# The feed-forward part of a gated state-space block in a new order on all engines

## What is computed

```
d_t, B_t, C_t = projections of u = silu(conv(in_proj @ ctx))     # per item
state = state * exp(d_t * A) + (d_t * u_t) * B_t                 # 16 state rows, over 256 positions
y     = (sum over the rows of state * C_t + D * u) * silu(norm(x))
x2    = x + tanh(g_xattn) * y
h     = act_quant(norm(x2))
inter = silu(h @ Wgate') * (h @ Wup')                            # 1024 wide
out   = x2 + tanh(g_ffn) * act_quant(fwht(inter)) @ Wdown'
```

## Time and profile before

| | |
|---|---|
| median of 3 runs | 265.46 us (264.85 to 266.59) |
| the profiled execution | 265.58 us, of which 263.8 us is the span from first to last instruction |
| busy share of the span: PE, DVE, ACT, POOL | 71%, 81%, 60%, 56% |
| mean granted clock of PE | 0.883 of full speed |

### The profile page before, as it was taken

How to read it: one execution, slowest core, us unless ns; L and a number is a source line. 1 busy time by engine, 2 the same in 40 slices (tenths; PEclk the granted TensorE clock), 3 DMA queues, 4 the chain that set the end, 5 groups by cost and what they waited for, 6 DMA issues and landing times. The chain is left out here.

```text
span 263.8 us, 3694 instructions
## 1 busy us (share of the span) xinstructions
PE 187.3 (71%) x1209; PEld 155.8 (59%) x1216; DVE 213.9 (81%) x340; ACT 157.3 (60%) x271; POOL 147.5 (56%) x213
## 2 busy tenths in 40 slices
PE   3779489895595569867667787675596768474945
PEld 2547388794494468647557666564485547342944
DVE  4489997898989499579989897998959775579872
ACT  1685996949234556994776799735748504650040
POOL 1100890999961096039999942999930399008500
PEclk9999855899779559999997999999979988989597
DMA  3891000000000000000000000000000000000001
GB/s 60 268 363 75 1 4 0 0 1 2 0 0 2 0 0 1 2 1 0 0 2 0 0 20 4 20 4 0 0 0 24 0 20 2 0 0 1 20 22 40
DMA packets 8149, 6.34 MB, mean 24 GB/s; under 512 B 2202, under 2 KB 7874, under 8 KB 8130
## 3 DMA queue, kind: packets, MB, share of 16 engines
q1 hardware_dynamic: 7154, 6.02, 7.1%
q10 hardware_dynamic: 976, 0.09, 0.3%
...
...
## 5 line engine op out<-in xcount | busy, mean ns | idle before, releaser
L1105 POOL TENSOR_SCALAR driveT<-duT,BT 128x256 f32<-128x256 f32 x120 | 62.2, 538 | 41.0 <-issue 21.3
L823 ACT ACTIVATE decay<-delta,zero_c,aneg 128x255 f32<-128x255 f32 x128 | 65.2, 589 | 1.7 <-DVE delta L1254 1.6
L1230 DVE TENSOR_TENSOR_SCAN state<-decay,BC 128x512 f32<-128x512 f32 x30 | 36.4, 1213 | 4.4 <-issue 4.3
L1272 DVE TENSOR_TENSOR prod<-state,BC 128x1024 f32<-128x1024 f32 x32 | 38.5, 1204 | 0.6 <-issue 0.6
L463 PE MATMUL PY<-id,prod 128*128 128x128 f32 x256 | 37.9, 297 | 1.4 <-DVE x L1294 1.0
L1230 DVE TENSOR_TENSOR_SCAN state<-decay,UP 128x512 f32<-128x512 f32 x30 | 35.8, 1193 | 0.0
L463 PEld LDWEIGHTS PY<-id,prod 128*128 128x128 f32 x256 | 32.8, 154 | 2.5 <-issue 1.2
L447 PE MATMUL BC<-bc,sel 96*128 96x256 bf16 x64 | 13.1, 288 | 27.4 <-DVE prod L1272 27.3
L1130 POOL TENSOR_TENSOR wnat<-wnat 128x512 f32<-128x512 f32 x18 | 22.9, 1274 | 15.9 <-DVE wnat L1352 15.2
L933 ACT COPY hT<-GP 128x1024 f32<-128x1024 f32 x8 | 8.1, 1010 | 35.0 <-PE GP L612 35.0
L407 PE MATMUL BC<-id,driveT 128*128 128x128 f32 x120 | 21.2, 305 | 10.9 <-POOL driveT L1105 10.8
...
## 6 DMA issues: line engine op xcount, KB each, us to landing
...
```

What stands on the lines that cost most here:

```text
L823: last = nc.scalar.activation(decay[:, m % RING, h, n, 1:L], delta[:, b % 2, h, 1:L], ACT.Exp, bias=zero_c[:], scale=aneg[:, h, NB * j + n ...
L1105: last = nc.gpsimd.tensor_scalar(driveT[:, m % RING, c, n], duT[:, b % 2, c], BT[:, b % 2, c, NB * j + n:NB * j + n + 1], 1.0, ALU.mult, A ...
L1230: nc.vector.tensor_tensor_scan(state[:, g % STATES, h].rearrange("p n l -> p (n l)"), decay[:, g % RING, h].rearrange("p n l -> p (n l)"), ...
L1272: nc.vector.tensor_tensor(prod[:, g % RING].rearrange("p h n l -> p h (n l)"), state[:, g % STATES].rearrange("p h n l -> p h (n l)"), PC. ...
```

## The change

The order of each engine's loop is written anew; no arithmetic is changed.

- In steps 3 to 5 PE does gate 0, up 0, gate 1, up 1, so `up(f, t)` waits for the silu of its own tile, and `gate(f, 1)` waits for `gate_times_up(f, 0)`. On DVE `gate_times_up(f, 0)` and `(f, 1)` go from the middle of steps 5 and 6 to the end of steps 4 and 5, and POOL's folds from steps 5, 6, 7 to 4, 5, 6.
- `inter_T(f, 0)` goes to PE's step 6, and `hadamard_mm(f, 0)` from step 0 of the next item to step 7. `absmax2(p, 0)` goes from step 1 to step 0, `round_down(p, 0)` from the start of step 2 to that of step 1, `q2_T(p, 0)` from 2 to 1. `hadamard_mm(p, 1)` stands ahead of `C_rows` in step 2, where it stood at the end of the step, and `absmax2(p, 1)` ahead of the scans of step 3, where it stood behind them.
- POOL makes driving terms LEAD = 5 steps ahead; the ring stays at 4. The pieces of `softplus_tail` and two of `weight_scale` stand a little earlier.
- ACT does `rstd2(f)` at the end of step 0 ahead of `softplus`, `copy_duT` in step 3 ahead of `for_silu`, `q2_out_early(p, 1)` between the two silus, `inter_out(f, 0)` in step 6.
- PE does `x_dbl(n)` in step 5, one step earlier, and of `in_proj` for n = 3 one half in step 1 and one in step 2, where they stood in 2 and 3.
- In the tail `absmax2(p, 0)` stands ahead of `residual`, and `round_down`, `q2_out`, `q2_T` of (2, 0) ahead of the tokens of item 3.
- Some PSUM banks and the waits that go with them are others.

The diff, cut to its core (helpers, PE's loop, then ACT's, POOL's, DVE's), shifted to the left:

```diff
+LEAD = 5
...
 def duT_bank(n):
-    return bank4 if n == 1 else X
+    return {1: bank4, 2: bank5}.get(n, X)
 def dt_bank(n):
     return bank5 if n < 2 else X
 def gateT_bank(k):
-    return bank6 if k == 0 else X
+    return bank6 if k <= 1 else X
...
...
         else:
             pe.wait_ge(dve_qT, 1)
         if f == 0 and t == 0:
-            pe.wait_ge(dve_wT, 6)
-            pe.wait_ge(act_duT, 2)
+            pe.wait_ge(act_duT, 3)
         elif f < B - 1 and t == 0:
             pe.wait_ge(act_tq, LC * f)
         elif f < B - 1:
-            pe.wait_ge(act_sg, LC * f + 1)
+            pe.wait_ge(dve_mul, LC * f + 1)
         elif t == 0:
             pe.wait_ge(act_tp, LC * f)
         else:
-            pe.wait_ge(act_tq, LC * f - 1)
+            pe.wait_ge(dve_scan, HALF * B * STEPS)
+            pe.wait_ge(dve_out, LC * (B - 2))
         tokens_by(f, t, wgT, pe_gate)
     def up(f, t):
-        if f == B - 1:
-            pe.wait_ge(act_sg, LC * f + t + 1)
-        elif t == 0:
-            pe.wait_ge(act_sg, LC * f + 2)
-        else:
-            pe.wait_ge(dve_mul, LC * f + 1)
+        pe.wait_ge(act_sg, LC * f + t + 1)
         tokens_by(f, t, wuT, pe_up)
...
         if DVE_DRIVES <= g + 2 < B * STEPS:
             drive_rows(g + 2, 0)
             drive_rows(g + 2, 1)
+        if s == 2:
+            if old:
+                hadamard_mm(p, 1)
         if s == 3:
             if new:
                 tokens_T(f)
-        if s == 4:
-            if new:
-                gate(f, 1)
         if g + 1 < B * STEPS:
             C_rows(g + 1)
         accumulate(g)
         if s == 0:
-            if k == 0:
-                dt_proj(1)
+            if k < B - 1:
+                dt_proj(k + 1)
+            if k == 0:
                 gate_T(0)
-            if 1 <= k < B - 1:
-                dt_proj(k + 1)
-            if old:
-                hadamard_mm(p, 0)
         if s == 1:
             if k == 0:
                 weight_sum()
+            if old:
+                inter_T(p, 1)
             if k >= 1:
                 gate_T(k)
             if old:
-                inter_T(p, 1)
+                q2_T(p, 0)
+            if k == 1:
+                in_proj(n, 0)
         if s == 2:
-            if old:
-                q2_T(p, 0)
             if front:
-                in_proj(n, 0)
-            if old:
-                hadamard_mm(p, 1)
+                in_proj(n, k)
         if s == 3:
-            if k == 0:
-                du_T(1)
+            if k < B - 1:
+                du_T(k + 1)
+            if new:
+                gate(f, 0)
             if old:
                 down(p, 0)
-            if new:
-                gate(f, 0)
-            if front:
+            if k == 0:
                 in_proj(n, 1)
+            if new:
+                up(f, 0)
         if s == 4:
-            if 1 <= k < B - 1:
-                du_T(k + 1)
-            if new:
-                up(f, 0)
             if old:
                 q2_T(p, 1)
+            if new:
+                gate(f, 1)
+                up(f, 1)
         if s == 5:
             if k == 0:
                 weight_T(0)
                 weight_T(1)
-            if new:
-                up(f, 1)
             if old:
                 down(p, 1)
+            if front:
+                x_dbl(n)
         if s == 6:
             if k == 0:
                 weight_T(2)
                 weight_T(3)
-            if front:
-                x_dbl(n)
+            if new:
+                inter_T(f, 0)
         if s == 7:
             if k == 0:
                 weight_T(4)
                 weight_T(5)
             if new:
-                inter_T(f, 0)
+                hadamard_mm(f, 0)
 p, f = B - 2, B - 1
-hadamard_mm(p, 0)
 inter_T(p, 1)
+hadamard_mm(p, 1)
+q2_T(p, 0)
 tokens_T(f)
-hadamard_mm(p, 1)
 gate(f, 0)
-q2_T(p, 0)
 gate(f, 1)
 up(f, 0)
 up(f, 1)
...
                 softplus(1)
                 gate_out(0)
             if new:
-                rstd2(f)
-            if old:
-                quant_down(p, 0)
-            if new:
                 second_norm(f)
         if s == 2:
             if new:
...
                 tokens_out_early(f)
             if old:
                 quant_down(p, 1)
-        if s == 4:
-            if k == 0:
-                copy_duT(1)
-        if s == 5:
-            if old:
-                q2_out_early(p, 1)
-        if s == 7:
-            if front:
-                dt_rows(n)
-                copy_BT(n)
-                high_pieces(n)
         if g + AHEAD < B * STEPS:
             decays(g + AHEAD)
         if s == 0:
+            if old:
+                quant_down(p, 0)
+            if new:
+                rstd2(f)
             if 1 <= k < B - 1:
                 softplus(k + 1)
         if s == 1:
...
             if old:
                 q2_out_early(p, 0)
         if s == 3:
+            if k < B - 1:
+                copy_duT(k + 1)
             if new or k + 1 < B:
                 for_silu()
             if new:
...
                 silu_u(n)
             if k + 1 < B:
                 silu_z(k + 1)
+            if old:
+                q2_out_early(p, 1)
             if new:
                 silu_gate(f, 1)
             for_exp()
-        if s == 4:
-            if 1 <= k < B - 1:
-                copy_duT(k + 1)
+        if s == 6:
+            if new:
+                inter_out(f, 0)
         if s == 7:
-            if new:
-                inter_out(f, 0)
+            if front:
+                dt_rows(n)
+                copy_BT(n)
+                high_pieces(n)
 p, f = B - 2, B - 1
+quant_down(p, 0)
 rstd2(f)
 for_silu()
 second_norm(f)
+inter_out(p, 1)
 scale_tokens(f)
-inter_out(p, 1)
-quant_down(p, 0)
 silu_gate(f, 0)
 quant_down(p, 1)
 silu_gate(f, 1)
...
 last.then_inc(pool_diag, 1)
 drives(DVE_DRIVES)
 norm_z(0)
-for m in range(DVE_DRIVES + 1, AHEAD):
+for m in range(DVE_DRIVES + 1, LEAD):
     drives(m)
 for k in range(B):
     p, f, n = k - 2, k - 1, k + 2
     old, new, front = p >= 0, f >= 0, n < B
     for s in range(STEPS):
         g = STEPS * k + s
-        if s == 2:
-            if 1 <= k < B - 1:
-                softplus_tail(k + 1, pool, nc.gpsimd, pool_front_link, 1)
         if s == 3:
-            if 1 <= k < B - 1:
-                softplus_tail(k + 1, pool, nc.gpsimd, pool_front_link, 2)
-        if g + AHEAD < B * STEPS:
-            drives(g + AHEAD)
+            if k == 0:
+                weight_scale(1)
+                weight_scale(2)
+        if g + LEAD < B * STEPS:
+            drives(g + LEAD)
         if s == 1:
             if k == 0:
                 pool_front_link.begin(pool, 0)
...
             if 1 <= k < B - 1:
                 pool_front_link.begin(pool, k)
                 softplus_tail(k + 1, pool, nc.gpsimd, pool_front_link, 0)
+                softplus_tail(k + 1, pool, nc.gpsimd, pool_front_link, 1)
         if s == 2:
+            if 1 <= k < B - 1:
+                softplus_tail(k + 1, pool, nc.gpsimd, pool_front_link, 2)
             if k == 0:
                 weight_scale(0)
             if k + 1 < B:
                 norm_z(k + 1)
-        if s == 3:
-            if k == 0:
-                weight_scale(1)
-                weight_scale(2)
-        if s == 5:
+        if s == 4:
             if new:
                 fold_tile(f, 0, 0)
                 fold_tile(f, 0, 1)
                 fold_tile(f, 0, 2)
-        if s == 6:
+        if s == 5:
             if new:
                 fold_tile(f, 1, 0)
                 fold_tile(f, 1, 1)
-        if s == 7:
+        if s == 6:
             if new:
                 fold_tile(f, 1, 2)
...
         if s == 1:
             if k == 0:
                 split(1)
-        if s == 2:
             if old:
                 round_down(p, 0)
         if s == 3:
             if new:
                 round_tokens(f)
+            if old:
+                absmax2(p, 1)
         if s == 4:
             if old:
                 round_down(p, 1)
...
         if g + 1 < B * STEPS:
             scan(g + 1, 0)
             scan(g + 1, 1)
-        if s == 1:
-            if old:
-                absmax2(p, 0)
-            if new:
-                second_rstd(f, dve_ln_link)
-        if s == 2:
-            if k == 0:
-                weight_means()
-            if new:
-                token_scale(f, dve_ln_link)
-        if s == 3:
-            if old:
-                absmax2(p, 1)
-        if s == 4:
-            if old:
-                result(p, 0)
-        if s == 5:
-            if new:
-                gate_times_up(f, 0)
-        if s == 6:
-            if k == 0:
-                weight_out(0)
-                weight_out(1)
-            if new:
-                gate_times_up(f, 1)
-            if old:
-                result(p, 1)
-        if s == 7:
-            if k == 0:
-                weight_out(2)
-                weight_out(3)
         if s == 0:
             if k == 1:
                 weight_out(4)
```

(36 more changed lines are left out.)

26 lines of the change are left out of this document (13 added, 13 removed).

## The result

The changed kernel took 271.74 us (median of 4 runs, 270.52 to 275.35; the 275.35 is an execution in a slower state that some executions fall into, and is left out of the ratio) against 266.02 us for the kernel before (median of 4, 264.85 to 267.90): a ratio of 1.019, 95% interval 1.011 to 1.028. It is slower by 5.7 us; the forecast was 262.6 us, with a range to 267.0. The profiled execution took 271.37 us, its span is 269.6 us.

The account below looks back on a forecast made before the run. DVE was taken to set the loop's time, the tail being one chain over all engines. Terms 3.1 + 3.5 + 1.2 - 2.7 + 1.2 - 1.1 - 2.2 = 3.0 off 265.58 gave 262.6 us, range 258.5 to 267.0.

Parts of the forecast that it names:

- Item 0 and step 9: POOL's earlier weight scalings and PE's earlier `x_dbl` in item 0 gain 3.1 us; `rstd2(0)` ahead of softplus gains 3.5.
- Steps 11 to 13: Item 1's new gate, silu, up order: `gate_times_up` waits 3.05 and 0.45 us, 3.5 against 4.6 before; gain 1.2.
- Items 2 and 3: DVE's waits in these items, with transform and feed-forward moved, rise from 9.2 to 11.9 us: loss 2.7.
- Contention: DVE roundings slowed beside POOL in items 2 and 3: half of 2.3 us excess goes, gain 1.2.
- Clock: One of four `hadamard_mm` in the loop runs at 1.2 GHz instead of 2.4: loss 1.1 us.
- rival 1: All four loop transforms (`hadamard_mm`) and the `accumulate` ahead of each run at half clock: 269.7 us, chance 0.13.
- two slow transforms: Sign for the half-clock transform case: `hadamard_mm` takes over 3 us more than once in the loop.
- Tail: Behind step 31, `residual` starts 6.9 us after the last product, 3.5 later; later order gives back 1.3: loss 2.2.
- Rival 3: First tile of items 2 and 3 waits 3.05 us for silu and up, as in item 1: 266.4 us, chance 0.12.
- Rival 4: POOL gains nothing by a lead of five with four ring buffers; 1.65 us lost: 264.2 us, chance 0.08.
- rival 2: Better case: contention goes wholly and PE's clock holds in loop and tail: 258.9 us, chance 0.22.
- Wrong if the loop ends later than 214: Sign of failure: the loop was forecast to end near 210 us instead of 216.5.

Follow-up runs that it names:

- a1_rstd_alone: The kernel before with only `rstd2(f)` moved to the end of ACT's step 0, ahead of softplus: 262.24 us against 265.54, ratio 0.984.
- the filled waits: The changed kernel with 4 or 8 unread products on PE ahead of its wait for each silu: 271.92 us, ratio 1.025 to the kernel before.
- after_absmax_back: The changed kernel, its own tail kept, with `absmax2(p, 1)` of step 3 behind the scans again: 270.0 us, ratio 1.016 to the kernel before.

## Why the prediction was wrong

It said 262.6 us in its sum against the profiled 265.58; the profiled execution took 271.37. The 8.8 us between divide into -0.9, +5.4, +4.5 and about -0.15, in the order of its steps:

- **Item 0 and step 9: gain 6.6, measured 7.5.** Right in size. At step 9 the product starts at 86.04, forecast 86.7; there is no wait for the square root. `a1_rstd_alone` shows the greater part (4.0 at step 9). The share of item 0 is not as firm: the same code shows 0.85 to 4.4 us of lead at step 8. Nor did its 3.9 us come as forecast. 2.8 were there at step 3, ahead of every weight rounding, and `a1_rstd_alone`, with item 0 unchanged, has 2.0 there. The rounding did end 1.1 us behind POOL's second scaling (62.49 after 61.39), as the forecast had it from the row; but DVE came to it at 59.89 and not at 61.8, and so it still took 2.60 us, and the next one 2.14 for 1.51. The wait of 1.22 us ahead of the scan of step 8 is gone, as forecast. That the sum fits is partly luck.
- **Steps 11 to 13: gain 1.2, measured a loss of 4.2.** This step failed by size. Its chain up to silu was right; its waits of 3.05 and 0.45 were 4.75 and 2.43, since PE was taken at full clock while the same sum made it wait twice. `up` took 1.89 us for the 0.9 assumed, and the driving rows and `accumulate`, ahead of the second gate, 1.9 us more than at full clock. The two waits are 3.7 us over the forecast, and the filled waits take 2.75 of these away. Of the other 1.7 us, 1.0 is lost between steps 9 and 11, ahead of the first tile: the rounding of the tokens took 1.16 us for 0.44 before, and it did so in `a1_rstd_alone` too, which loses 0.7 us there. So it is there without the new order of gate and up. The rest is in small waits, and 4.6 less 3.5 is 1.1, not the 1.2 of the sum.
- **Items 2 and 3: loss 2.7 - 1.2 + 1.1 = 2.6, measured 7.1.** Its miss of 4.5 us would have turned the sign by itself, as the 5.4 of item 1 would; this one an experiment takes back. The forecast took `absmax2(p, 1)` ahead of the scans as its own wait (0.7 us, measured 0.38 and 0.52). It didn't ask who waits for the scans behind it, although it says of the waiting `gate_times_up` that the driving rows and a scan stand behind. Here `tokens_T` stood behind those rows, and the tokens, silu, `up` and `gate_times_up` behind it. Two pairs of runs show the edit to be worth 7.0 and 8.4 us, in both directions. Of the smaller terms, `absmax2` tile 0 at 1.7 was right (1.88 twice), `round_down` 1.3 was 1.65; `gate_times_up` 1.4 and 0.8 was 1.66 and 2.69 in item 2, 0.9 and 0.8 was 1.19 and 1.03 in item 3; the wait for rounding tokens, taken as nothing, was up to 1.5.
- **Contention, +1.2.** Half right: the eight roundings of L1353 took 6.2 us in all after 6.8, but that of the tokens of item 1 grew by 0.7. The risk was larger than its bounds say: in four later kernels one `round_down` alone took 2.83 to 2.90 us.
- **Clock, -1.1 and rival 1.** The place was wrong, the price near. Rival 1 gave 269.7 and saw the transform at half clock. No transform in the loop ran so, as the group of its products shows (ns, least, median, most):

```profile
L628 PE MATMUL GP<-had,hT x80: 275/275/275, 122.7 to 225.4; 128*128 128x128 f32 x80
```

  It was the products behind PE's wait for silu that ran at 1.2 GHz. The sign that the forecast gave for rival 1, two slow transforms, did not appear, so the rival did not hold either; that its time is within 2 us of the result is chance. By the Trainium skill, TensorE: Matmul & The Clock Gate, "What's actually happening", the clock follows how busy PE has been; the trace agrees in item 2, where `accumulate` took 1.90 us behind a wait of 2.95 and 1.04 without it. The forecast cited that and then applied it to one instruction only.
- **Tail: loss 2.2, measured 2.05.** Right in size against the kernel before: the residual 7.1 us after the last product's end (forecast 6.9), `gate_times_up(3, 0)` 16.0 behind it (14.9). The table shows that the loss is more than it looks: the old tail took 3.4 us less behind the same order of the loop (50.5 against 47.1), 5.1 with `absmax2` put back.
- **Rival 3** (silu and up a round trip for each tile, 266.4) is the rest of the truth: item 2 waits 1.66 and 2.69, not 3.05 twice. **Rival 4** (LEAD does nothing) is not decided by these runs; **rival 2** did not occur.
- "Wrong if the loop ends later than 214": the last product ended at 220.3.

What stays open: why the tail behind `gate_times_up(3, 0)`, the same instructions, takes 26.2 us in the changed kernel and 28.4 in `after_absmax_back`. The products there show both levels of the clock, but which wait sets them was not tried. Open too is what puts POOL's run of driving terms later against DVE in some kernels than in others.
